# Value product of a key tile over all query columns in one piece, in three attentions of a four-layer kernel

## The chip, the core and the metric

The kernel runs on one core of a Trainium2 chip. The core has five engines that run side by side, each through its own queue in order: TensorE (PE, matrix products; PEld are its weight loads), VectorE (DVE), ScalarE (ACT), GpSimd (POOL) and SyncE (SP, which here only issues DMAs). TensorE writes its results to PSUM, eight banks of 512 float32 columns on each of 128 partitions, and the other engines read them from there. The metric is the time of one execution on the device in microseconds.

## The reference, cut to what matters

The input is x of 8 batches, 512 tokens and 128 channels. Four layers, each a mixer and a feed-forward part, are applied with a layer norm ahead and a residual behind each. The mixers of layers 0, 1 and 3 are attentions with 16 heads of 8 channels; layer 1's is causal, with rotary embedding; layer 3's masks two corner scores:

```python
scores = jnp.einsum('bhqd,bhkd->bhqk', q, k) * scale
attn = jax.nn.softmax(scores, axis=-1)
out = jnp.einsum('bhqk,bhkd->bhqd', attn, v)
out = jnp.transpose(out, (0, 2, 1, 3)).reshape(B, T, C) @ w_out + b_out
```

The rest (two mixtures of experts with sorted tokens, a small attention over 8 rows, a state-space layer, gated low-rank experts in layer 3) is not touched.

## The kernel before

`attention_all` is called three times, with the tags `a0_`, `a1_` (causal) and `a3_`. It handles the 8 batches as one stream of work. Its units are: a batch, four groups of four heads in a batch (32 groups `g` in all), four key tiles of 128 keys (`kt`) in a group, four heads in a key tile. A key tile's scores for one head are one product of 128 keys by 512 queries (causal: 512, 384, 256 or 128 queries for the four tiles). Scores are numbered `n`, 16 in a group; two heads of a pair use the two halves of TensorE's rows and are issued together.

For a pair of scores these things happen:

- **M**, line 1030: the same products with queries and keys exchanged, from which VectorE takes the maxima of each query (line 478). M has two sets of two banks in turn. Line 1049 transposes the maxima of a group, ScalarE negates them (897), and a DMA places them as one more row of the queries (line 1011), so that the scores come out with the maximum taken off.
- **S**, line 1077: the two scores, each into one of three banks `Sc` that are used in turn. ScalarE takes the exponential of each (line 887) into `prob`, which has room for 12.
- **V**, line 1104: the value product of a key tile, float32, one for each of the four heads of the group, on four column strips of TensorE of 32 columns each, so that the four run beside one another. It accumulates over the key tiles in one further bank. A float32 product shows in the trace as two instructions.

In the causal attention M and S have masking products of 64 columns behind them (lines 1035, 1039, 1083, 1086).

The order on each engine is made by `take_turns`: every generator yields the place, a number, at which its next piece stands, and the pieces of all generators are issued by rising place. The units count scores: M stands at every even number, S at the even number `n` plus 0.3, V of key tile `a` at `4 * a + 6.5`; its second half stands 2.0 later, or 0.05 later for a group's last key tile. Between them stand the projections of the next batch (turn 338, Q and K 1133, value 1137), the transposes of outputs (1118), the output's (338) and its projection (1147). In `a3_` layer 3's feed-forward part (`gated`) and the mixing of the expert outputs (`mixed`) run in the same stream.

A score bank may be written again when it has been read. This is the rule, and the order of the pair:

```python
def s_free(pe, u):
    if s_place[u] >= 3:
        pe.wait_ge(S("s_read"), s_place[u] - 2)
```

`tensor_scores` calls it ahead of each of the two scores of a pair. The turned inputs, the Q and K projections and the transposed maxima use the same three banks; M, the value projection, the output transposes and the output projection use M's two sets. How V is cut is told by `value_halves`, which returns the ranges of query columns; `tensor_values` issues one piece for each range.

Of the kernel before, what the change touches and what calls it, by code (L numbers as in the profile page):

```python
# [22 lines left out]
B, T, C = 8, 512, 128  # L23
# [156 lines left out]
def build(nc, x, pa, pb, pc, pd, pk, pkb, w1e, w2e, wa3, wb3, unused, out):  # L180
    top = ExitStack()
    with top:
# [164 lines left out]
        def attention_all(tag, xres, w, scale, causal=False, corners=False, swapped=None, double=None, bo=None,  # L347
# [4 lines left out]
            with ExitStack() as ctx:  # L352
# [110 lines left out]

                def value_halves(kt):
                    q0 = first_query[kt]
                    return [(q0, T)] if T - q0 <= 256 else [(q0, (q0 + T) // 2), ((q0 + T) // 2, T)]

                def tri_table(name, lo):
                    return kb(name)[lo:lo + HALF, :]
# [619 lines left out]
                def tensor_values(pe):  # L1089
                    for a in range(16 * B):  # L1090
                        g, kt = divmod(a, NT)
                        b = g // NG
                        spans = value_halves(kt)
                        for half, (q0, q1) in enumerate(spans):
                            yield 4 * a + 6.5 + half * (0.05 if kt == NT - 1 else 2.0)
                            if half == 0:
                                s_done(pe, ("score", 4 * a + 3))
                                if kt == 0:
                                    if g % NG == 0:
                                        m_done(pe, ("v", b))  # L1100
                                    if g % 2 == 0 and g:
                                        pe.wait_ge(S("av_taken"), g // 2)
                            for hl in range(GH):
                                i = pe.matmul(V[32 * hl:32 * hl + 32, q0:q1], vaug[:, b % 3, kt, g % NG * GH + hl, :],  # L1104
                                              prob[:, (4 * a + hl) % DEEP, q0:q1], start=kt == 0 and half == 0 and g % 2 == 0,
                                              stop=kt == NT - 1 and g % 2 == 1,
                                              skip_group_check=True)
                            if half == len(spans) - 1:
                                i.then_inc(S("av_done"), 1)
# [1665 lines left out]
```

## Time and profile before

| | |
|---|---|
| median of 3 runs | 2944.87 us (2943.6 to 2948.09) |
| profiled execution | 2956.76 us, span 2955.0 us, 48935 instructions |
| PE busy | 2235.5 us (76%) |
| DVE, ACT, POOL busy | 2013.7 (68%), 1537.1 (52%), 1232.6 us (42%) |
| V, line 1104 | 5632 instructions, 434.2 us busy |
| maxima, line 478 (DVE) | 768 instructions, 806.0 us busy |
| exponentials, line 887 (ACT) | 1536 instructions, 744.6 us busy |
| mean granted clock of TensorE | 0.861 |

Busy time is the time in which an engine has at least one instruction of the group under way; instructions of TensorE overlap, and so do the beginning and end of two that follow on another engine. So the distance from one start to the next says more than a duration. The times in the rows below are counted from the start of the span. "idle before <- releaser" in square brackets is the time in which the engine stood still and the instruction that ended it.

### The profile page before, as it was taken

The page shows a single profiled execution, that of the slowest core. Times are in us where ns is not written, and L with a number is a line of the kernel's source. Part 1 is how long each engine was busy: PE and PEld are TensorE (multiplying, and loading weights), DVE is VectorE, ACT ScalarE, POOL GpSimd, SP SyncE. Part 2 cuts the span into 40 slices and gives each one's busy share as a digit, 9 for nine tenths or more (in the row PEclk, how much of TensorE's full clock was granted, in tenths as well). Part 3 has the DMA queues.
Part 4 walks back from the last instruction along what each step waited for, and adds up shares of the span by engine and source line. Part 5 has one row for each costly group of instructions (what it writes and reads, how often), then busy time and mean ns, then how long its engine had stood idle before and what let it go on. Part 6 is the DMA issues. An engine that isn't in the chain of part 4 may idle for free. (4 is left out here: it accounts for less than half of the span.)

```text
span 2955.0 us, 48935 instructions
## 1 busy us (share of the span) xinstructions
PE 2235.5 (76%) x17390; PEld 1137.2 (38%) x17406; DVE 2013.7 (68%) x3639; ACT 1537.1 (52%) x3073; POOL 1232.6 (42%) x1267
## 2 busy tenths in 40 slices
PE   4899996887899996664846777877722985889886
PEld 1233333444344443553732333333322982233332
DVE  5789876786565663554246889889863226888884
ACT  3678882111465654332436777666420223767775
POOL 3342403443443420332354666766754443442310
PEclk9999997777899998776877988898955997999998
DMA  3311100000111111001950000000003981222210
GB/s 102 99 27 42 30 16 0 1 1 1 23 39 40 43 36 54 25 21 28 300 176 0 1 0 1 0 0 1 1 29 98 299 273 39 44 40 50 44 30 15
DMA packets 127481, 152.80 MB, mean 52 GB/s; under 512 B 19976, under 2 KB 108616, under 8 KB 126632
## 3 DMA queue, kind: packets, MB, share of 16 engines
q1 hardware_dynamic: 120648, 136.12, 17.1%
q0 software_dynamic: 6592, 13.56, 1.3%
q8 instruction: 140, 2.29, 0.3%
q14 instruction: 101, 0.83, 0.1%
HBM read 96.15 MB, written 25.59 MB: 41 GB/s over the span
## 5 line engine op out<-in xcount | busy, mean ns | idle before, releaser
L478 DVE TENSOR_REDUCE a_mx<-banks 128x2 f32<-128x1024 f32 (+3 forms) x768 | 806.0, 1087 | 240.5 <-PE banks L1039 127.0
L887 ACT ACTIVATE a_prob<-banks 128x512 f32<-128x512 f32 (+3 forms) x1536 | 744.6, 541 | 277.3 <-PE banks L1077 155.0
L1104 PE MATMUL banks<-a_prob,a_vaug 128*32 128x256 f32 (+2 forms) x5632 | 434.2, 390 | 0.2
L2210 POOL TENSOR_TENSOR m_hc<-m_h,m_cs 128x512 f32<-128x512 f32 x256 | 332.2, 1320 | 132.1 <-DVE m_h L2075 126.2
L1077 PE MATMUL banks<-a_Qs,a_Ks 64*128 64x512 bf16 (+3 forms) x1536 | 326.4, 366 | 52.9 <-DMA a_Qs<-a_negm 30.1
L2075 DVE TENSOR_TENSOR_SCAN m_h<-banks,m_u 128x512 f32<-128x512 f32 x256 | 301.1, 1210 | 21.1 <-issue 21.1
L1030 PE MATMUL banks<-a_Ks,a_Qs 63*128 63x512 bf16 (+3 forms) x1536 | 285.0, 368 | 37.7 <-DVE a_mx L478 30.3
L2358 PE MATMUL banks<-m_hc,kc 128*128 128x512 f32 x512 | 292.5, 656 | 9.6 <-DVE m_yf L2192 8.5
L2266 ACT ACTIVATE banks<-m_dt,acoef 128x512 f32<-128x512 f32 x256 | 174.9, 688 | 137.5 <-DVE m_h L2075 136.6
L1030 PEld LDWEIGHTS banks<-a_Ks,a_Qs 63*128 63x128 bf16 x1536 | 74.2, 93 | 331.9 <-issue 163.7
L1104 PEld LDWEIGHTS banks<-a_prob,a_vaug 128*32 128x32 f32 x5632 | 119.1, 109 | 156.6 <-issue 115.4
L1077 PEld LDWEIGHTS banks<-a_Qs,a_Ks 64*128 64x128 bf16 x1536 | 109.6, 95 | 142.8 <-ACT a_prob L887 71.6
L2060 DVE TENSOR_TENSOR m_u<-m_dtx,banks 128x1024 f32<-128x1024 f32 x128 | 153.9, 1203 | 5.9 <-PE banks L2333 3.2
L1319 POOL TENSOR_TENSOR a_room<-a_room 128x512 f32<-128x512 f32 x72 | 100.3, 1405 | 108.5 <-ACT a_room L1331 107.7
L2358 PEld LDWEIGHTS banks<-m_hc,kc 128*128 128x128 f32 x512 | 107.0, 211 | 78.9 <-issue 47.4
L2333 PE MATMUL banks<-m_G,kb 96*128 96x512 bf16 x128 | 53.9, 421 | 96.9 <-ACT m_cs L2256 83.6
L818 POOL TENSOR_SCALAR a_small<-a_mom 128x4 f32<-128x4 f32 x24 | 5.5, 228 | 261.5 <-DVE a_mom L551 261.5
L1921 POOL DMA_INDIRECT rows_back<-c_ob,c_yb x71 | 68.0, 957 | 110.5 <-DVE c_ob L1986 110.2
L1962 ACT ACTIVATE c_hb<-banks 128x512 f32<-128x512 f32 x71 | 42.4, 597 | 125.1 <-PE banks L1940 88.3
L1348 PE MATMUL banks<-a_hT,w_a 128*128 128x512 f32 x144 | 95.6, 779 | 2.5 <-ACT a_room L1331 2.5
L2256 ACT ACTIVATE m_cs<-banks 128x512 f32<-128x512 f32 x128 | 74.8, 584 | 40.4 <-PE banks L2344 39.4
L1331 ACT ACTIVATE a_room<-banks 128x512 f32<-128x512 f32 x72 | 43.0, 597 | 92.5 <-PE banks L1348 80.9
(429 smaller groups left out, 4240.5 us busy)
## 6 DMA issues: line engine op xcount, KB each, us to landing
c_wbuf<-in_w2e SPq DMA_DIRECT2D x71, 512.0 KB
b_wbuf<-in_w1e SPq DMA_DIRECT2D x39, 578.0 KB
a_Ks<-a_parts SPq DMA_DIRECT2D x252, 64.0 KB
a_Qs<-a_parts SPq DMA_DIRECT2D x252, 64.0 KB
rows_in<-in_unused SPq DMA_DIRECT2D x1, 4579.5 KB, 17.7
c_yb<-rows_in SPq DMA_DIRECT2D x71, 64.5 KB
a_mixed_in<-rows_back SPq DMA_DIRECT2D x16, 256.0 KB, 4.3
a_Qs<-a_negm SPq DMA_DIRECT2D x192, 2.0 KB
```

The source lines that it names most:

```text
L478: dve.tensor_reduce(both[:, :, c], m_bank(u)[:, :, 0:keys[c % NT]], AX.X, ALU.max).then_inc(S("m_read"), 1)
L887: act.activation(prob[:, n % DEEP, first_query[kt]:T], s_bank(u)[:, first_query[kt]:T], ACT.Exp, scale=scale).then_inc(S("s_read"), 1)
L1030: i = pe.matmul(bank[:, par, 0:keys[j]], Qs[lo:lo + LAST, b % 4, pair, q:q + P], Ks[lo:lo + LAST, b % 4, pair, 0:keys[j]], start=True, sto ...
L1077: i = pe.matmul(s_bank(u)[:, q0:T], Ks[lo:lo + HALF, b % 4, pair, kt * P:(kt + 1) * P], Qs[lo:lo + HALF, b % 4, pair, q0:T], start=True, s ...
L1104: i = pe.matmul(V[32 * hl:32 * hl + 32, q0:q1], vaug[:, b % 3, kt, g % NG * GH + hl, :], prob[:, (4 * a + hl) % DEEP, q0:q1], start=kt == ...
L1319: gp.tensor_tensor(hid[:, c, :], relu[:, c % 2, :], relu[:, c % 2, :], ALU.mult).then_inc(S("squared"), 1)
L1348: pe.matmul(bank[:, 1 + c % 2, :], w, hT[:, :], start=True, stop=True).then_inc(S("hidden"), 1)
L2060: dve.tensor_tensor(u[:, k % 3], dtx[:, b % 2], R[:, k % 2, :].unsqueeze(1).broadcast_to([P, NCH, T]), ALU.mult).then_inc(S("u_ready"), 1)
L2075: dve.tensor_tensor_scan(h[:, n % 4, :], A[:, c, :], u[:, (k - 1) % 3, c, :], 0.0, ALU.mult, ALU.add).then_inc(S("scanned"), 1)
L2210: gp.tensor_tensor(hc[:, n % 6, :], h[:, n % 4, :], cs[:, k % 4, :], ALU.mult).then_inc(S("weighed"), 1)
L2266: act.activation(A[:, c, :], dt[:, b % 2, c, :], ACT.Exp, scale=acoef[:, c * DS + k % DS:c * DS + k % DS + 1]).then_inc(S("decayed"), 1)
L2358: pe.matmul(Y[:, c, :], ident, hc[:, (NCH * k + c) % 6, :], start=n == 0, stop=n == DS - 1, skip_group_check=True).then_inc(S("summed"), 1)
```

## The change

```diff
                 def value_halves(kt):
                     q0 = first_query[kt]
-                    return [(q0, T)] if T - q0 <= 256 else [(q0, (q0 + T) // 2), ((q0 + T) // 2, T)]
+                    return [(q0, T)]
```

The value product of a key tile is now one piece over all its query columns: 512 in `a0_` and `a3_`, 512 or 384 for the first two key tiles in `a1_`, whose other two were one piece before. The piece stands where the first half stood. The other engines' orders are the same.

TensorE in a plain stretch of the first attention (from one V to the next but one; `a0_prob` and `a0_vaug` are V's operands). Before:

```order
L1104 MATMUL banks<-a0_prob,a0_vaug 32x256 x4
L1030 MATMUL banks<-a0_Ks,a0_Qs 128x512 x2
L1077 MATMUL banks<-a0_Qs,a0_Ks 128x512 x2
L1104 MATMUL banks<-a0_prob,a0_vaug 32x256 x4
L1030 MATMUL banks<-a0_Ks,a0_Qs 128x512 x2
L1077 MATMUL banks<-a0_Qs,a0_Ks 128x512 x2
```

The same stretch after:

```order
L1104 MATMUL banks<-a0_prob,a0_vaug 32x512 x4
L1030 MATMUL banks<-a0_Ks,a0_Qs 128x512 x2
L1077 MATMUL banks<-a0_Qs,a0_Ks 128x512 x2
L1030 MATMUL banks<-a0_Ks,a0_Qs 128x512 x2
L1077 MATMUL banks<-a0_Qs,a0_Ks 128x512 x2
```

The second V group has moved up into the first, and two pairs of M and S now follow one another.

TensorE where the Q and K projections of the next batch stand (line 1133, the first one Q, the second K). Before:

```order
L1104 MATMUL banks<-a0_prob,a0_vaug 32x256 x4
L1133 MATMUL banks<-a0_hT,w_a 128x512
L1030 MATMUL banks<-a0_Ks,a0_Qs 128x512 x2
L1077 MATMUL banks<-a0_Qs,a0_Ks 128x512 x2
L1104 MATMUL banks<-a0_prob,a0_vaug 32x256 x4
L1133 MATMUL banks<-a0_hT,w_a 128x512
L1030 MATMUL banks<-a0_Ks,a0_Qs 128x512 x2
L1077 MATMUL banks<-a0_Qs,a0_Ks 128x512 x2
L1104 MATMUL banks<-a0_prob,a0_vaug 32x256 x4
```

After:

```order
L1077 MATMUL banks<-a0_Qs,a0_Ks 128x512 x2
L1133 MATMUL banks<-a0_hT,w_a 128x512
L1030 MATMUL banks<-a0_Ks,a0_Qs 128x512 x2
L1077 MATMUL banks<-a0_Qs,a0_Ks 128x512 x2
L1104 MATMUL banks<-a0_prob,a0_vaug 32x512 x4
L1133 MATMUL banks<-a0_hT,w_a 128x512
L1030 MATMUL banks<-a0_Ks,a0_Qs 128x512 x2
L1077 MATMUL banks<-a0_Qs,a0_Ks 128x512 x2
```

The Q projection now stands between two score pairs, the K projection directly behind a V.

## Rows read from the trace of the kernel before

**Rows 1.** Stretches of the three attentions: length, then busy us (instructions), PEclk, DMA.

```profile
66.00:446.00 380.00, 349.06 (x3303) 121.04 (x3307) 310.76 (x367) 300.53 (x583) 115.04 (x154) 0.97 0.19 43
777.00:1143.00 366.00, 332.94 (x4819) 166.91 (x4815) 224.49 (x367) 226.76 (x595) 123.17 (x103) 0.93 0.17 37
2501.00:2922.00 421.00, 374.05 (x3401) 131.92 (x3401) 353.87 (x618) 318.23 (x631) 141.14 (x181) 0.96 0.21 39
```

**Rows 2.** Order of time, plain steps of a0: start, length, engine, line, what.

```profile
358.40 4.62 DVE L478 TENSOR_REDUCE a_mx<-banks 128x2 f32<-128x1024 f32 x4 [0.37 <-PE banks L1030]
...
358.51 0.64 PE L1104 MATMUL banks<-a_prob,a_vaug 128*32 128x256 f32 x8
...
359.08 0.39 PE L1030 MATMUL banks<-a_Ks,a_Qs 63*128 63x512 bf16 x2
...
359.31 0.41 PE L1077 MATMUL banks<-a_Qs,a_Ks 64*128 64x512 bf16 x2
...
360.75 0.64 PE L1104 MATMUL banks<-a_prob,a_vaug 128*32 128x256 f32 x8
```

**Rows 3.** Order of time, two halves of a group's last key tile, with transposed maxima.

```profile
329.70 1.07 PE L1104 MATMUL banks<-a_prob,a_vaug 128*32 128x256 f32 x16
...
330.70 0.39 PE L1030 MATMUL banks<-a_Ks,a_Qs 63*128 63x512 bf16 x2
```

**Rows 4.** Order of time, two adjacent halves after the last maxima of a0.

```profile
438.06 1.07 PE L1104 MATMUL banks<-a_prob,a_vaug 128*32 128x256 f32 x16
...
439.07 0.60 PE L1077 MATMUL banks<-a_Qs,a_Ks 64*128 64x512 bf16 x3
439.55 3.60 ACT L887 ACTIVATE a_prob<-banks 128x512 f32<-128x512 f32 x7 [0.39 <-PE banks L1077]
...
440.20 0.39 PE L1077 MATMUL banks<-a_Qs,a_Ks 64*128 64x512 bf16 x1 [0.53 <-ACT a_prob L887]
...
440.52 0.64 PE L1104 MATMUL banks<-a_prob,a_vaug 128*32 128x256 f32 x8
...
441.50 0.64 PE L1104 MATMUL banks<-a_prob,a_vaug 128*32 128x256 f32 x8
```

**Rows 5.** Order of time, output transpose of one batch and the next, a0 and a3.

```profile
323.75 0.66 PE L338 MATMUL banks<-kc,a_onorm 128*128 128x128 f32 x4
...
370.56 0.66 PE L338 MATMUL banks<-kc,a_onorm 128*128 128x128 f32 x4
...
2613.56 0.66 PE L338 MATMUL banks<-kc,a_onorm 128*128 128x128 f32 x4
...
2669.31 0.55 PE L338 MATMUL banks<-kc,a_onorm 128*128 128x128 f32 x3
```

**Rows 6.** Order of time, a projection of a0 and what follows.

```profile
347.79 1.12 PE L1133 MATMUL banks<-a_hT,w_a 128*128 128x512 f32 x2
348.85 0.39 PE L1030 MATMUL banks<-a_Ks,a_Qs 63*128 63x512 bf16 x2
```

**Rows 7.** Order of time, TensorE waiting for maxima in a3.

```profile
2626.08 0.39 PE L1030 MATMUL banks<-a_Ks,a_Qs 63*128 63x512 bf16 x2 [0.79 <-DVE a_mx L478]
```

**Rows 8.** Order of time, a causal group of a1 and the end of its batch.

```profile
936.55 0.64 PE L1104 MATMUL banks<-a_prob,a_vaug 128*32 128x256 f32 x8
...
937.36 0.27 PE L1077 MATMUL banks<-a_Qs,a_Ks 64*128 64x256 bf16 x2
...
937.78 0.66 ACT L887 ACTIVATE a_prob<-banks 128x256 f32<-128x256 f32 x2 [0.27 <-PE banks L1086]
...
938.73 0.53 PE L1104 MATMUL banks<-a_prob,a_vaug 128*32 128x192 f32 x8
...
940.39 0.42 PE L1104 MATMUL banks<-a_prob,a_vaug 128*32 128x256 f32 x4
...
944.07 0.39 PE L1077 MATMUL banks<-a_Qs,a_Ks 64*128 64x512 bf16 x2 [2.72 <-DMA a_Qs<-a_negm]
```

**Rows 9.** Busy time and clock in the last steps of a0, columns as in rows 1.

```profile
431.00:446.00 15.00, 14.39 (x150) 5.00 (x152) 0.85 (x3) 14.05 (x29) 0.00 (x0) 1.00 0.01 1
```

## The prediction

> **What bounds the kernel now.** I read first the busy time of each engine in the stretches of the three attentions that call the changed helper (`a0_`, `a1_`, `a3_`; I call them the first, the causal and the last attention) [rows 1]. TensorE is busy 92%, 91% and 89% of them, VectorE 82%, 61% and 84%, ScalarE 79%, 62% and 76%. Three engines are close together in the first and the last, so a share of busy time does not say which ends last; the order of time does.
>
> In a plain stretch of the first attention [rows 2] one step (two scores of a head pair) is: maxima product (M) 0.23 us until the next group starts, score pair (S) 0.32, from what the other two leave of 1.12, half of the value product (V) 0.57 (358.51 to 359.08). Two steps, that is one key tile, take 2.24 (358.51 to 360.75). VectorE runs four maxima in 4.62, 1.13 to 1.15 apart, so it is as late as TensorE. ScalarE's exponentials, when queued, start 0.50 apart (seven in 3.60 in [rows 4]), two in 1.0: it has 0.12 us per step to spare. TensorE and VectorE bound this stretch together, and ScalarE is fed evenly.
>
> The changed thing can be seen in the trace already: the last key tile of every group of four heads is issued as two halves with nothing between them, 16 instructions that hold TensorE 1.00 us until the next group (329.70 to 330.70) [rows 3], and once per attention this comes without a transpose or a maxima product around it, at 438.06 [rows 4]. In that place the next two pairs are issued behind it, four score products. The first three start from 439.07 on; the fourth waits 0.53 us for an exponential and starts at 440.20, and the next V at 440.52. V to V is 2.46 us, where the steps with halves beside it run 0.98 (440.52 to 441.50): 1.96 for two. **A whole value product there costs 0.50 us more than two halves apart.**
>
> **Why, as a loop.** A score may be written to its PSUM bank when the third-last score (three banks) has been read by ScalarE. Call the four scores between two whole V's C, D, E, F. F needs C's bank. From the rows: C is issued 1.01 after V's start; ScalarE starts on it 0.48 later (439.07 to 439.55), and F starts 0.65 after that (440.20), when it has been read, 1.13 after C; V stands behind F on TensorE's queue and starts 0.32 later. So V to V = 1.01 + 1.13 + 0.32 = 2.46, a chain through two engines in which nothing can be ahead. With halves C is issued one whole step before F's turn (1.12 + its place in the pair), so C is read just as F comes up. During the whole product ScalarE runs dry; after it TensorE waits for ScalarE.
>
> **The change part by part.**
> It removes work from TensorE: per key tile of 512 queries 2 x 0.57 becomes 1.00 us, 0.14 less; per causal tile of 384 queries 2 x 0.46 (the 0.53 of [rows 8] less the 0.07 by which 0.64 overlaps what follows in [rows 2]) becomes about 0.78 (0.14 of switching and 0.64 of streaming, 3/4 of the 0.86 of a 512 one), 0.14 less. Whether 8 instructions of 512 columns cost what 16 of 256 do has no row. Nearest are the 16 adjacent ones, 1.00; the length grows evenly with the columns elsewhere (0.46 for 192, 0.57 for 256), so I take 1.00, with bounds 0.90 and 1.14 (two halves apart). Changed are 3 of 4 key tiles in the first and last attention (96 each) and 2 of 4 in the causal one (64). Half of the weight loads go; they overlap already and I count nothing.
> It moves work: the second half stood one step later, behind the next M and S. Nobody waits longer for its result: the buffers it frees are due six scores later, and the last tile of a group was adjacent before. So the whole price is the gap that it tears between score pairs.
>
> *First attention.* With M between V and C, a plain key tile becomes 2.46 + 0.22 = 2.68 us instead of 2.24: **+0.44**. VectorE needs about 2.26 per key tile and is no longer last. One batch is 16 key tiles; it is 46.81 us long, read between two output transposes (323.75, 370.56) [rows 5]. Of its 16 intervals from V to V:
> - 4 follow a last key tile, which was whole before: 0.
> - 8 are plain: +0.44, one of them only +0.26 as VectorE's statistics had already stretched it: 3.3. The one with the output projection: +0.43.
> - the Q projection (1.06 us [rows 6]) stands between C, D and E, F, so it fills the wait: 2.24 + 1.06 becomes 2.10 + 1.06: -0.14.
> - the K projection stands between V and C. It hides nothing, and ScalarE's copy of it (0.69) delays C by 0.1: +0.55.
> - the value projection stands there too, but in the kernel before it waited 0.4 for VectorE: +0.05.
> Sum 3.3 + 0.43 - 0.14 + 0.55 + 0.05 = **4.2 us per batch**. Seven batches 29.5; the last has no projections for a next one and ends without maxima (2.46 for 1.96, five times): 5. In all **+34**.
>
> *Last attention.* The batch is 55.75 us long [rows 5], and 9 us more of it are VectorE's: TensorE waits 0.79 for maxima at 2626.08 behind its statistics [rows 7]. In the intervals of its two normalisations, of the gate and of ScalarE's normalisation (five of the plain eight) VectorE or ScalarE ends last in both kernels and a longer interval hides: 0 to +0.04, one about -0.1. Left are three plain ones (+0.42 each, 1.3), K +0.55, Q -0.14, rest 0: **1.7 per batch**. Five middle batches 8.5; the first, without gate work, 3; the last two, without next projections and with less of VectorE's, 3 and 4.5. In all **+18**, rounding down.
>
> *Causal attention.* Pieces are shorter [rows 8]. After the whole V of the first key tile (936.55) C and D are 256 wide, ScalarE starts 0.42 after C (937.36 to 937.78) and one takes about 0.38 (two in 0.66), so F may start 0.86 after C and V 0.26 later: 1.00 + 0.24 + 1.12 = 2.36 against 2.18 (936.55 to 938.73): +0.18. After the second, with 0.78 for V and scores of 128, by the same steps 1.82 against 1.66 (938.73 to 940.39): +0.16. Per batch four groups, of which in one the K projection fills the wait: some 1.0 us (3 x 0.18 - 0.14 + 4 x 0.16), 8 for all. Each batch also ends in a wait for the DMA that places the maxima, 2.72 us at 944.07; it takes in part of what comes shortly before it, so **+6**.
>
> **Sum**: 34 + 18 + 6 = 58 us. The profiled execution took 2956.76 us (span 2955.0 and 1.8 around it), which gives 3014.8; the median of the runs is 2944.87, 11.9 less, and on it the forecast is **3003 us**, 2.0% slower. With V at 0.90 the loop is 0.1 shorter, some 18 us less over about 180 intervals in which it ends last; with 1.14, 25 more.
>
> **The rivals.**
> *A, faster: TensorE's saving counts.* If exponentials kept ahead of the scores, the removed 96 x 0.14 x 2 + 64 x 0.14 = 36 us would come off wherever TensorE ends last. For it speak the 89 to 92%; against it VectorE at 1.13 a step (most of it could not be used in the plain stretches) and above all the 0.53 wait in rows 4. About 25 us: 2920. Chance 0.08. The Trainium skill (TensorE: Matmul & The Clock Gate, Back-to-back issue gap) has a stream run at the columns over the clock and 2.5 ns a matmul; as an estimate by it, merging saves 8 x 2.5 = 20 ns per key tile, 4 us in all, and says nothing of the wait. The row shows 0.14.
> *B, no change:* the new waits are taken in by VectorE everywhere, as in the last attention's gated part. VectorE's own 2.26 per key tile is 0.4 short of that. 2945, chance 0.04.
> *C, slower, but only in part:* the loop is as I say in the first attention, and the last and the causal one hide it. 34, less the start of the first attention, where a large DMA holds it up anyway (8): 26 us, 2971. Chance 0.18.
> *D, slower by more:* the last attention pays like the first (34) and the causal one hides nothing (12): 80 us, 3025. Chance 0.12.
> *E, the clock falls.* Evenly spread idle of half a microsecond in 2.7 could bring the granted clock down. At the end of the first attention, with just such waits, it is 1.00 (2.4 GHz) over 15 us [rows 9]; the causal attention with its waits is at 0.93. If the first and last went from 0.97 and 0.96 to 0.90, 7% of 800 us is 56 more, of which some two thirds lie on the chain: 3040. Chance 0.07. The Trainium skill (same page, A second HAM failure mode: psum-queue depth-cycling) reports such micro-idle between groups that cycle through PSUM banks as a cause of a clock that swings; by that rule this rival would be the forecast. Rows 9 speak against it.
>
> **Numbers.** Forecast 0.51 (3003), C 0.18, D 0.12, E 0.07, A 0.08, B 0.04. Slower by over 0.2% (about what a measurement of this kernel can tell from no change) 0.88, within it 0.04, faster 0.08. The range 2964 to 3026 holds the forecast, C and D and leaves A, B and E out.
>
> **What would show it.** In the profile after: a V group of 8 instructions with 512 columns, about 1.00 us to the next group; score pairs alternately 0.55 apart and behind V; between C and F 1.13, with idle before the second score of the pair, released by line 887 (some 0.5 us, about 180 times, where there were few such waits); batches of 51.0 in the first and about 57.4 us in the last attention; VectorE idle in front of every second maxima. If the waits for line 887 don't grow, or the first attention is not at least 20 us longer, the loop is wrong; if PEclk in it falls under 0.95, rival E is in it.

## The result

| | before | after |
|---|---|---|
| median of 5 runs | 2944.87 us | 2987.98 us (2985.06 to 2992.83) |
| ratio | | 1.0146, 95% interval 1.0132 to 1.0160 |
| profiled execution | 2956.76 us | 2992.83 us |
| span | 2955.0 us | 2991.0 us |

The changed kernel is 43 us, 1.5%, slower; forecast was 58 us slower, with a range of 19 to 81. The page of its profile:

```profile
span 2991.0 us, 43831 instructions
...
PE 2240.0 (75%) x14846; PEld 1075.5 (36%) x14846; DVE 2016.6 (67%) x3639; ACT 1526.5 (51%) x3073; POOL 1228.0 (41%) x1267
...
L1104 PE MATMUL banks<-a_prob,a_vaug 128*32 128x512 f32 (+3 forms) x3072 | 379.6, 567 | 0.2
```

TensorE issues 2560 instructions fewer and V is busy for 379.6 us in place of 434.2, a saving of 55 us by that row alone. The kernel is slower all the same, so what V itself saves does not decide the time.

The plain stretch of the first attention, in order of time (start, length, engine, line, what; in brackets the idle time ahead and what ended it); it answers to [rows 2]:

```profile
399.35 0.39 PE L1077 MATMUL banks<-a_Qs,a_Ks 64*128 64x512 bf16 x1 [0.31 <-ACT a_prob L887]
399.67 1.06 PE L1104 MATMUL banks<-a_prob,a_vaug 128*32 128x512 f32 x8
...
400.67 0.39 PE L1030 MATMUL banks<-a_Ks,a_Qs 63*128 63x512 bf16 x2
...
400.89 0.38 PE L1077 MATMUL banks<-a_Qs,a_Ks 64*128 64x512 bf16 x2
401.10 2.36 DVE L478 TENSOR_REDUCE a_mx<-banks 128x2 f32<-128x1024 f32 x2 [0.31 <-PE banks L1030]
...
401.37 2.06 ACT L887 ACTIVATE a_prob<-banks 128x512 f32<-128x512 f32 x4 [0.60 <-PE banks L1077]
...
402.02 0.39 PE L1077 MATMUL banks<-a_Qs,a_Ks 64*128 64x512 bf16 x1 [0.31 <-ACT a_prob L887]
...
402.33 1.07 PE L1104 MATMUL banks<-a_prob,a_vaug 128*32 128x512 f32 x8
```

It reads as the loop was told. V holds TensorE 1.00 us (399.67 to 400.67). The pair C, D is issued at 400.89, ScalarE has run dry meanwhile (0.60 idle) and starts at 401.37, 0.48 later; the fourth score starts at 402.02, 1.13 after C; the next V at 402.33. V to V is 2.66 us where it was 2.24. All three engines stand still once per key tile.

Where the 36 us between the two profiled executions are, read from the end of the first maxima product to the start of the last output transpose of each attention:

| stretch | before | after | difference |
|---|---|---|---|
| first attention | 402.6 | 428.2 | +25.6 |
| causal attention | 387.3 | 388.6 | +1.3 |
| last attention | 447.8 | 464.6 | +16.8 |
| between the first and the causal | 308.8 | 309.3 | +0.5 |
| between the causal and the last | 1332.5 | 1324.3 | -8.2 |

The first three make 43.7, close to the 43.1 between the medians. The stretch of 1330 us between the causal and the last attention has the same instructions in all kernels here and took between 1316.7 and 1332.5 us in their profiled executions; its -8.2 is within that scatter, and it is why a comparison of two single executions shows 36.

### The profile page after: what moved, and what is told of

Same layout as the page of the kernel before. It is cut to its first block and busy times, and to the rows that moved or that the text cites. A ratio compares the mean times of both kernels' runs of the same rounds, so it can differ in the third digit from the quotient of the medians.

```text
span 2991.0 us, 43831 instructions
## 1 busy us (share of the span) xinstructions
PE 2240.0 (75%) x14846; PEld 1075.5 (36%) x14846; DVE 2016.6 (67%) x3639; ACT 1526.5 (51%) x3073; POOL 1228.0 (41%) x1267
## 5 line engine op out<-in xcount | busy, mean ns | idle before, releaser
L887 ACT ACTIVATE a_prob<-banks 128x512 f32<-128x512 f32 (+3 forms) x1536 | 735.3, 545 | 324.5 <-PE banks L1077 212.5
L1077 PE MATMUL banks<-a_Qs,a_Ks 64*128 64x512 bf16 (+3 forms) x1536 | 391.1, 367 | 83.4 <-ACT a_prob L887 54.4
L1104 PE MATMUL banks<-a_prob,a_vaug 128*32 128x512 f32 (+3 forms) x3072 | 379.6, 567 | 0.2
L2075 DVE TENSOR_TENSOR_SCAN m_h<-banks,m_u 128x512 f32<-128x512 f32 x256 | 300.8, 1207 | 21.1 <-issue 21.1
L1030 PE MATMUL banks<-a_Ks,a_Qs 63*128 63x512 bf16 (+3 forms) x1536 | 287.1, 368 | 33.4 <-DVE a_mx L478 28.2
```

Of the source, the lines that this page charges most:

```text
L887: act.activation(prob[:, n % DEEP, first_query[kt]:T], s_bank(u)[:, first_query[kt]:T], ACT.Exp, scale=scale).then_inc(S("s_read"), 1)
L1030: i = pe.matmul(bank[:, par, 0:keys[j]], Qs[lo:lo + LAST, b % 4, pair, q:q + P], Ks[lo:lo + LAST, b % 4, pair, 0:keys[j]], start=True, sto ...
L1077: i = pe.matmul(s_bank(u)[:, q0:T], Ks[lo:lo + HALF, b % 4, pair, kt * P:(kt + 1) * P], Qs[lo:lo + HALF, b % 4, pair, q0:T], start=True, s ...
L2075: dve.tensor_tensor_scan(h[:, n % 4, :], A[:, c, :], u[:, (k - 1) % 3, c, :], 0.0, ALU.mult, ALU.add).then_inc(S("scanned"), 1)
```

## Experiments

Each group of experiments ran on one chip with its own runs of the kernel before, so times are compared as ratios to those. 1.0146 is whole V in all three attentions.

| kernel | ratio to the kernel before | 95% interval |
|---|---|---|
| e1, whole V in first and last attention | 1.0164 | 1.0143 to 1.0185 |
| e2, whole V in the causal attention | 1.0028 | 1.0015 to 1.0042 |
| e3, halves, all adjacent | 1.0146 | 1.0124 to 1.0168 |
| e4, whole V, half of the maxima moved | 1.0118 | 1.0098 to 1.0139 |
| e5, halves, half exponentials | 0.9922 | 0.9893 to 0.9952 |
| e6, whole V, half exponentials | 1.0007 | 0.9992 to 1.0023 |
| e7, halves apart in more places | 0.9977 | 0.9961 to 0.9994 |
| e8, whole V in the causal attention but for its last batch | 0.9989 | 0.9973 to 1.0004 |
| e9, whole V in the causal attention's last batch alone | 1.0010 | 0.9998 to 1.0023 |
| e10, e7 and e8 together | 0.9974 | 0.9963 to 0.9985 |

### Is it the place or the size of the instruction?

```diff
-                            yield 4 * a + 6.5 + half * (0.05 if kt == NT - 1 else 2.0)
+                            yield 4 * a + 6.5 + half * 0.05
```

> V stays in halves of 256 or 192 columns, 16 instructions, but the second half stands directly behind the first for every key tile, where the whole product stands. Theory (only the place counts, and what the gap between score pairs does): same time as whole V, 2988 within 4 us, V group 1.00 us to the next. Rival (the size of the instruction counts, a 512-column product or its writes to PSUM being slower): 2945 to 2955.

Ratio 1.0146, the same as whole V. In order of time, TensorE:

```profile
392.16 1.07 PE L1104 MATMUL banks<-a_prob,a_vaug 128*32 128x256 f32 x16
...
394.51 0.39 PE L1077 MATMUL banks<-a_Qs,a_Ks 64*128 64x512 bf16 x1 [0.31 <-ACT a_prob L887]
394.83 1.07 PE L1104 MATMUL banks<-a_prob,a_vaug 128*32 128x256 f32 x16
```

V to V is 2.67, with 16 short instructions as with 8 long ones. The instruction's size costs and saves nothing that can be seen here; what costs is that nothing stands between the halves. Three engines share these intervals; the next two experiments ask which of them makes the loop. A fourth score bank, which would test the number of banks directly, was not run: M's four banks, the three of the scores and V's one are all eight.

### Is the exponential in the loop?

```diff
-                        act.activation(prob[:, n % DEEP, first_query[kt]:T], s_bank(u)[:, first_query[kt]:T],
-                                       ACT.Exp, scale=scale).then_inc(S("s_read"), 1)
+                        end = T if n < DEEP else (first_query[kt] + T) // 2
+                        act.activation(prob[:, n % DEEP, first_query[kt]:end], s_bank(u)[:, first_query[kt]:end],
+                                       ACT.Exp, scale=0.0).then_inc(S("s_read"), 1)
```

The same edit on the kernel before (e5) and on the changed one (e6). It leaves out half of each exponential, so both have another output than the reference.

> V in halves; from the 13th score of each attention on, ScalarE takes the exponential of the first half of the query columns only (256 of 512), and all with scale 0, so the output is not the reference's. An exponential then takes 0.38 us in place of 0.60. Theory: with halves the exponential does not end last, plain key tiles stay at 2.24 to 2.26 us (TensorE, VectorE); the four intervals behind adjacent halves lose up to 0.4. About 2930 to 2945 where the kernel before has 2945.

> V whole, with the same cut of the exponentials as in the run with halves. Theory: the loop (1.01 + 0.22 from V to the next pair, 0.48 until ScalarE starts, 0.38 exponential, 0.06, 0.32 to V) is 2.47 us in place of 2.67, so the difference of whole against halves falls from 43 us to about half, 20 to 25. Rival (TensorE's or VectorE's order costs, ScalarE does not): the difference stays 43 us.

The two differ by 1.0007 - 0.9922 = 0.0085, 25 us, where the full exponentials leave 43. By the two intervals it is 15 to 35, so a difference that had stayed at 43 is ruled out. It was forecast as 20 to 25. The kernel with halves gained 23 us, where 0 to 15 were expected: besides the intervals behind adjacent halves (2.73 in place of 3.16) its last batches, which have no maxima and which ScalarE bounds, are shorter. The loop in e6, TensorE and ScalarE (line numbers are one higher there):

```profile
389.14 1.07 PE L1105 MATMUL banks<-a_prob,a_vaug 128*32 128x512 f32 x8
...
390.36 0.38 PE L1078 MATMUL banks<-a_Qs,a_Ks 64*128 64x512 bf16 x2
...
390.80 0.86 PE L1078 MATMUL banks<-a_Qs,a_Ks 64*128 64x512 bf16 x2
390.84 1.24 ACT L888 ACTIVATE a_prob<-banks 128x256 f32<-128x256 f32 x4 [1.21 <-PE banks L1078]
391.59 1.06 PE L1105 MATMUL banks<-a_prob,a_vaug 128*32 128x512 f32 x8
```

2.45 us from V to V, 0.21 less, which is the shorter exponential (0.38 in place of 0.60); ScalarE still starts 0.48 after C and is idle for 1.21 per key tile. It is idle half of the time and in the loop nonetheless: what counts in it is how soon it has read a score, not how busy it is.

### Is the maxima product in the loop?

```diff
-                m_at = {("max", g, c): max_at(g, c) for g in range(NGB) for c in range(8)}
+                m_at = {("max", g, c): max_at(g, c) + (0.0 if c % 2 else 0.45) for g in range(NGB) for c in range(8)}
```

> V whole, and in every second step (the one without V) the maxima product M stands behind the score pair and not ahead of it. So the loop V, M, pair, exponential, fourth score loses M's 0.22 us: V to V 2.46 instead of 2.67 in plain key tiles, where TensorE waits for ScalarE longer instead of doing M. Theory: first attention -1.8 us per batch (8 plain intervals and the one with the output projection), -14; last attention -6; causal -6 to -10: about 2960. Rival (VectorE being fed in bursts is what costs): M moved further apart from its neighbour changes nothing or costs, 2985 to 3000.

Ratio 1.0118: 8 us less than whole V (1 to 15 by the two intervals), where 28 were forecast: a miss. In the first attention it did what was said:

```profile
392.57 1.06 PE L1104 MATMUL banks<-a_prob,a_vaug 128*32 128x512 f32 x8
...
393.57 0.39 PE L1077 MATMUL banks<-a_Qs,a_Ks 64*128 64x512 bf16 x2
393.79 0.78 PE L1030 MATMUL banks<-a_Ks,a_Qs 63*128 63x512 bf16 x4
394.05 2.06 ACT L887 ACTIVATE a_prob<-banks 128x512 f32<-128x512 f32 x4 [0.38 <-PE banks L1077]
394.41 0.68 PE L1077 MATMUL banks<-a_Qs,a_Ks 64*128 64x512 bf16 x2
395.02 1.06 PE L1104 MATMUL banks<-a_prob,a_vaug 128*32 128x512 f32 x8
```

The pair follows V at once, both maxima products stand where TensorE would wait, and V to V is 2.45; a batch is 49.03 us in place of 50.89, and the attention 416.0 in place of 428.2. The last attention got 1.7 us longer (466.3) and the causal one 3.7 (392.3), where 6 and 6 to 10 less were forecast. TensorE's waits for VectorE's maxima ahead of line 1030 rose there, from 25.2 to 33.4 us in the last attention and from 1.0 to 7.9 in the causal one: VectorE was given its input later, and in those intervals it ends last. So the loop is confirmed in the first attention; a fifth of a microsecond taken out of it is worth something only where the loop ends last.

### Which attention?

```diff
                 def value_halves(kt):
                     q0 = first_query[kt]
+                    if not causal:
+                        return [(q0, T)]
                     return [(q0, T)] if T - q0 <= 256 else [(q0, (q0 + T) // 2), ((q0 + T) // 2, T)]
```

> V is whole in the first and the last attention, in halves (as before) in the causal one. Theory (the loop through three score banks: whole V, next pair, its exponential, fourth score): nearly the whole loss is here, 24 + 17 us by the two traces, so +41 us on the kernel before, 2986. Rival (the loss is spread over all changed key tiles alike, 96 + 96 + 64): three quarters of 43, +32, 2977.

e2 has the same edit with `if causal`.

> V is whole in the causal attention alone. The loss there was forecast as +6 us; the trace after shows about +1 to the last output transpose: six batches with projections are shorter by 1.3 each, the last two longer by 0.9 and 4.6. Theory: +1 to +3 us, not to be told from no change. Rival (spread alike): +11 us.

e1 is 1.0164, 48 us, a little more than the 41 expected; the whole loss, 1.0146, lies within its interval. e2 is 1.0028, 8 us, more than the 1 to 3 expected. The two make 56 us where the whole change costs 43, and the intervals do not cover that gap; no run here explains it. The causal attention of e2 is 11.0 us longer (398.3 for 387.3), and 8.1 of it are the last batch, 39.2 for 31.1. Stretches of it (length, busy us and instructions of PE, PEld, DVE, ACT, POOL, then PEclk): first e2 up to and from 1135.7, then the kernel before over its last batch.

```profile
1119.00:1135.70 16.70, 14.88 (x219) 7.67 (x218) 10.60 (x15) 11.16 (x30) 0.00 (x0) 0.99 0.06 18
1135.70:1158.00 22.30, 18.60 (x145) 6.70 (x143) 1.23 (x5) 9.80 (x27) 0.00 (x0) 0.50 0.00 1
```

```profile
1114.50:1145.50 31.00, 27.16 (x419) 13.77 (x420) 12.60 (x20) 21.18 (x58) 0.00 (x0) 1.00 0.04 11
```

With whole V the granted clock falls to half, 1.2 GHz, 17 us into the last batch (not at its start, as my expectation of e8 has it), at the start of its third group, and does not come back before the end; with halves it stays at 2.4 GHz over the whole batch. In the kernel after this comes later, at the start of the last group:

```profile
1162.80:1173.20 10.40, 7.88 (x61) 2.84 (x58) 0.85 (x3) 3.58 (x11) 0.00 (x0) 0.50 0.00 0
```

So two more kernels, with `value_halves` also given the batch `b`: whole V in the causal attention for all but its last batch (e8) and for the last alone (e9).

```diff
+                    if causal and b < B - 1:
+                        return [(q0, T)]
```

> V whole in the causal attention, but in halves in its last batch; the other attentions as before. In the run with the whole causal attention the last batch took 39.2 us in place of 31.1, and the granted clock of TensorE was at 1.2 GHz in it from the start; the batches with projections were shorter by 0.4 us each. Theory (the loss is the clock in the last batch): the +8 us on the kernel before are gone, -3 to +1. Rival (it is the loop, in all batches): +6 to +8.

> V whole in the last batch of the causal attention alone, 8 key tiles of 512 or 384 queries; all else as before. Theory (the clock falls in that batch once V is whole in it): +5 to +8 us, and in the trace the last batch 35 to 39 us long in place of 31.0 with the granted clock at 1.2 GHz in it. Rival (what fell there in the other runs came from how the batches ahead ended, or the loop alone costs): +1.5 us, last batch 32.5, clock 2.4 GHz.

e8: the 8 us are gone, the last batch is 31.0 us and its clock 1.00. e9: 1.0010, 3 us, with an interval from -1 to +7 that leaves both its theory (+5 to +8) and its rival (+1.5) open; in its profiled execution the clock fell at 1139.0, 11 us before the last output transpose, and the batch took 35.8 us, as the theory has it:

```profile
1139.00:1150.00 11.00, 8.40 (x66) 3.11 (x66) 0.85 (x3) 4.09 (x13) 0.00 (x0) 0.50 0.01 1
```

The clock fell in this batch in all four kernels traced that have whole V in it and full exponentials: 10 to 22 us before its end in e2, e9 and the kernel after, and for 6.8 us from 1155.2, 9.5 us before its end, in e4. With the halved exponentials (e6) it held, and in none of the kernels with halves apart (before, e1, e5, e7, e8, e10) did it fall. With 16 adjacent halves (e3) it held too and the batch took 32.6, which is the price of the loop without the clock. So not every kernel with that rhythm is caught; what decides it is open, and each kernel has one profiled execution, so whether the clock falls in all of its executions is not known. The Trainium skill (TensorE: Matmul & The Clock Gate, A second HAM failure mode: psum-queue depth-cycling) names short idle times between groups that cycle through PSUM banks as a cause of such falls. The four kernels in which the clock fell agree with it; e3 and e6 in this batch, and the first attention, with the same loop and a clock of 1.00 in its steady batches, do not.

### A version that beats both

[rows 3] show adjacent halves in the kernel before too, at every group's last key tile. If the loop is what they cost, the kernel before pays it 32 times in the first and 32 times in the last attention (the causal one has a single piece there). In odd groups the output copy waits for them; in even groups nothing does:

```diff
-                            yield 4 * a + 6.5 + half * (0.05 if kt == NT - 1 else 2.0)
+                            yield 4 * a + 6.5 + half * (0.05 if kt == NT - 1 and g % 2 else 2.0)
```

> V in halves as before, and in every even group the halves of the last key tile stand apart too (2.0 in place of 0.05). Theory: the interval that follows it (3.16 us, with the maxima's transpose in it) becomes 2.74, as the second half leaves ScalarE a pair earlier: 16 of them in each of the first and the last attention, some hidden by VectorE in the last, nothing in the causal one, where that tile has 128 columns and is one piece: -10 to -13 us, 2934. Rival (an adjacent pair costs nothing, only what stands between costs): +-2 us.

TensorE in that place:

```profile
327.99 0.64 PE L1104 MATMUL banks<-a_prob,a_vaug 128*32 128x256 f32 x8
...
329.10 0.64 PE L1104 MATMUL banks<-a_prob,a_vaug 128*32 128x256 f32 x8
...
330.11 0.69 PE L1077 MATMUL banks<-a_Qs,a_Ks 64*128 64x512 bf16 x2
330.72 0.64 PE L1104 MATMUL banks<-a_prob,a_vaug 128*32 128x256 f32 x8
```

327.99 to 330.72 is 2.73, forecast 2.74, before 3.16. Of the 0.86 a batch 0.7 stays (46.13 for 46.82), since the next interval with VectorE's statistics takes 0.2 back, and the last attention shows no gain (450.8 us in this execution, 447.8 before). Ratio 0.9977: 5 to 7 us, half of what was expected, and faster than the kernel before beyond its interval.

> Both edits that gave the fastest runs so far: halves of the last key tile apart in even groups, and V whole in the causal attention but for its last batch. Theory: the gains are at different places and add up, -5 to -7 and -3 to 0, so -5 to -10 us, 0.2% to 0.35% faster than the kernel before. Rival: the second was chance, -5.

0.9974, interval 0.9963 to 0.9985: 2939.13 against 2947.58 us, 8 us, as expected. That the second edit adds anything to the first can't be told from these runs.

## Why the prediction was right, point by point

**The mechanism and its size per key tile were right.** Median of the intervals from V to V in the traces:

| interval | before | forecast | after |
|---|---|---|---|
| plain, first attention | 2.24 | 2.68 | 2.67 |
| behind a last key tile | 3.16 | 3.16 | 3.16 |
| with the output projection | 4.28 | 4.71 | 4.71 |
| with the Q projection | 3.27 | 3.16 | 3.16 |
| with the K projection | 3.30 | 3.85 | 3.72 |
| with the value projection | 3.72 | 3.77 | 3.86 |
| causal, first key tile | 2.19 | 2.36 | 2.36 |
| causal, second key tile | 1.65 | 1.82 | 1.83 |

A batch of the first attention was forecast at 51.0 us and is 50.89, one of the last at 57.4 and is 58.06. That the first comes out so closely is in part luck: the interval with the K projection costs 0.42 more than before where 0.55 was forecast, the one with the value projection 0.14 where 0.05 was. The output transposes, which answer to [rows 5]:

```profile
336.58 0.66 PE L338 MATMUL banks<-kc,a_onorm 128*128 128x128 f32 x4
```

```profile
387.47 0.66 PE L338 MATMUL banks<-kc,a_onorm 128*128 128x128 f32 x4
```

```profile
2694.89 0.66 PE L338 MATMUL banks<-kc,a_onorm 128*128 128x128 f32 x4
```

```profile
2752.95 0.66 PE L338 MATMUL banks<-kc,a_onorm 128*128 128x128 f32 x4
```

**The first attention was over-sized: +25.6 for +34.** The term that was mis-sized is "seven batches 29.5": it multiplied a steady batch by seven, and the first three did not pay that. Differences between consecutive output transposes, before and after: 60.7 and 59.3, 47.8 and 50.9, three times 46.8 and 50.9, 42.5 and 47.6, 36.2 and 40.0. Up to the third transpose the change costs 4.6 us (2.8 up to the first, then -1.4 and 3.1), where the sum had 12.6; behind it 21.1, where the sum had 21.8. In the second batch the large DMA holds TensorE 8.5 us before and 6.0 after; the loop's loss hides in that wait, as rival C said and the sum did not.

**The causal attention: +1.3 for +6**, and for other reasons than told. Its intervals grew as forecast, 0.17 and 0.18, about 1 us a batch. But the DMA waits, which answer to the last of [rows 8], took in more than I allowed. TensorE's waits in it, before and then after (in total, times, longest):

```profile
PE banks L1077 <- DMA a_Qs<-a_negm: 19.7, 8, 3.4
```

```profile
PE banks L1077 <- DMA a_Qs<-a_negm: 13.0, 8, 2.6
```

6.7 us less. The other profiled executions agree: with halves in all batches but the last (e1, e7, e9) these waits are 18.8 to 20.4 us, with whole V (e2, e8, e10) 13.4 to 15.9. The time at 1.2 GHz ahead of the last batch is 27 us after and 48 before, but it can't be put down to the change: e1, whose causal attention is that of the kernel before, has 38. Nor is a loss seen ahead of the last batch. Up to the last transpose but one the stretch takes 356.2 us before and 352.9 after; with halves (e1, e7, e9) it takes 353.0 to 356.4, with whole V (e2, e8, e10) 355.2 to 359.1. The last batch is 4.6 us longer after and 8.1 in e2. By e3, in which the clock held, some 1.6 of it are the loop and the rest the clock. That is rival E, in a place where I had not looked for it; I had taken [rows 9] from the end of the first attention.

**The last attention: +16.8 for +18.** The size was right. From one transpose to the next the five batches behind the first transpose take 53.8, 55.7, 56.6, 56.3 and 55.1 us before and 56.5, 58.1, 58.1, 58.2 and 55.5 after, 8.8 more in all for the 8.5 of the sum; the start costs 1.3 for 3, the last two stretches 4.2 and 2.5 for 3 and 4.5. The steady batches scatter here more than in the first attention. The clock is at 1.2 GHz for 27 us in all in these five after, 6.8 in each of four, and for 20 before, 0 to 6.8 in each; whether the change has a part in that is not shown. Over 15 us there (2650 before, 2674 after):

```profile
2650.00:2665.00 15.00, 12.11 (x106) 3.44 (x102) 14.41 (x36) 9.78 (x21) 6.26 (x8) 0.89 0.17 39
```

```profile
2674.00:2689.00 15.00, 12.72 (x67) 2.65 (x66) 13.54 (x35) 8.62 (x19) 5.78 (x8) 0.77 0.18 42
```

**V at 1.00 us**: right, 399.67 to 400.67. **What would show it**: the wait before the pair's second score was there, with 0.31 us of idle in place of the 0.5 named, since the first score of the pair is still counted as busy behind the wait's start. TensorE's waits for the exponential in the whole kernel, before and then after (in total, times, longest):

```profile
PE banks L1077 <- ACT a_prob L887: 19.3, 59, 1.0
```

```profile
PE banks L1077 <- ACT a_prob L887: 54.4, 176, 0.6
```

That is 117 waits more, 73 of them in the first attention (16 and 89), where about 180 were named.

**The sum.** 58 us were forecast and 43 measured: 8 of the 15 between them are the start of the first attention, 5 the causal one, 1 the last.

**The rivals.** A (TensorE's saving counts) and B (no change) fell with the result. D (the last pays like the first) fell with +16.8. C had the right correction for the start of the first attention but too little of the rest. E was right for the end of the causal attention alone. In A, eight instructions fewer in each of the 256 changed key tiles make 5 us by the price given there and not 4; e3 and the kernel after show no difference between 8 and 16 instructions (1.00 us both).

## What to carry to other kernels

Where three buffers pass work between two engines that are both nearly full, count the loop, not the busy time: from one long piece on the producer to the next, through the first result that the consumer could not have had before it. Two short pieces with other work between them can beat one long piece that costs the producer less, and an existing place with the long form in the trace prices the change. When a loss per batch has been found, multiply it only over batches in which the loop ends last: a wait for a DMA or a slower engine next to it pays part of it back.

## What was not expected of the hardware

A 512-column and two adjacent 256-column float32 products on four column strips hold TensorE equally long, 1.00 us for the group of four heads: 8 or 16 instructions make no difference. The granted clock can fall to 1.2 GHz behind a stretch in which TensorE is 89% busy (14.88 of 16.70 us before 1135.7 in e2) with no wait longer than 0.3 us. It stayed at 2.4 GHz over 200 us of the first attention after, where TensorE is busy 89% too (177.43 of 200.00) and waits 0.3 us 46 times for an exponential and up to 0.9 us for maxima:

```profile
235.00:435.00 200.00, 177.43 (x1168) 49.99 (x1167) 165.52 (x192) 148.01 (x293) 51.01 (x72) 1.00 0.14 30
```

The busy share alone does not tell the two apart.
